# Three accumulators of softmax sums joined on POOL before TensorE reduces them

## The chip, the cores and the metric

The kernel runs on one core of a Trainium2 chip. The metric is the device time of one execution in microseconds (us). The engines are TensorE (PE; its weight loads are PEld), VectorE (DVE), ScalarE (ACT), GpSimd (POOL) and SyncE (SP, which here only issues DMAs).

## What is computed

A block of three residual steps on x of shape (2, 2048, 512), in float32: half a feed-forward layer with sign weights, self-attention with 16 heads of 32, half a feed-forward layer again. Each step normalizes first.

```python
def attn(x):                      # per batch element, 16 heads, HEAD_DIM 32
    q, k, v = proj(w_q), proj(w_k), proj(w_v)
    scores = einsum('bhqd,bhkd->bhqk', q, k) * SCALE
    probs = softmax(scores, axis=-1)
    attn = einsum('bhqk,bhkd->bhqd', probs, v)
    return einsum('bsd,ed->bse', attn, w_o)

x = x + 0.5 * ffn(layernorm(x))   # relu(x @ sign(up).T * up_scale) @ sign(down).T * down_scale
x = x + attn(layernorm(x))
x = x + 0.5 * ffn(layernorm(x))
```

## The kernel before

The stages follow each other: first feed-forward (up to about 620 us), projections to q, k, v (to about 865 us), attention (to about 2540 us), output projection and second feed-forward. The change lies in attention.

Attention runs over NH = 32 heads (16 for each of two batch elements), H in the code. A head has 2048 keys in KT = 16 tiles of 128 (kt) and 2048 queries in QC = 4 chunks of 512 (q). The work is written transposed: a score matmul (`scores`, L802) has 128 keys on the partitions and 512 queries along the row. ACT takes the exponential (L786, in `scalar_tile`) into a slot `prob[kt % 8]` of 128x2048; a slot is 1 MB, and there are PR = 8. The maxima that are subtracted come from a second matmul of the same size (`maxima`, L806), whose results DVE reduces (L737); this runs LEAD = 4 tiles ahead, so that tiles 12 to 15 of a head's loop already make maxima for the head after next. At tile TURN = 13 the maxima are transposed by PE (L822), split by DVE and written by SP into two rows of the q tile (`max_rows`).

The order on PE is written by hand in `tensor_group`: a group u is two key tiles, G = 2, so a head has 8 groups. A group is 8 score matmuls and 8 maxima matmuls in turn, and then the output matmuls (`out_tile`, L830) of the two tiles before: for each tile four matmuls with v, one for each chunk, 32 columns wide, which work side by side into the four quarters of one bank. The last two tiles of head H - 1 are thus multiplied in group 0 of head H.

Besides its output a head needs the sum of its probabilities over all keys. Three accumulators of 128x2048 share the 16 tiles: POOL adds tiles 0, 2, 4, ..., 14 and 15 into `acc` (`add`, L710); tiles 1, 5, 9, 13 go by DMA into the first of `dma_acc`, tiles 3, 7, 11 into the second (`move`: the first of each is a plain copy, L722, the later ones accumulate, L725). POOL issues these DMAs between its additions, in the order of the tiles, so they share one queue. ACT writes a slot again 8 tiles later and waits (`tile_free`) until the addition or the DMA that read it is done. The accumulators are double buffered by the parity of H.

What is left is the sum over the 128 partitions. PE makes it with a matrix of ones in `sums`: four matmuls on `acc` (L846) and four on each of the two DMA accumulators (L851). It runs once a head, for head H - 1, at the end of group SUMS_AFTER = 2 of head H. It takes one of the four banks that the maxima use in turn. ACT copies this bank to `head_total` (`copy_sums`, L228) at tile 6, after the second of the tile's four exponentials; PE may use the bank again only then (`bank_free`, semaphore `sums_copied`). SP sends the sums through DRAM to turn them (`move_sums`), DVE inverts them at tile 12 (`invert`, L255), SP stores them (`store_inverse`).

At the start of each head SP waits for the last output matmuls of the head before (`head_free`) and then loads q, k and v of head H + 2: four of q and k high parts, two low parts, and v, 256 KB each (L679, L681).

The last head (31) is different: fewer tiles on POOL and DMA, some tiles multiplied by ones directly (L837), and in between the first output projection products. There DVE, at tile 6, waits for `t_ready` of head 30 and then runs the first normalization steps of the last stage (L83, L85, L87, L89), which PE's mean matmuls at the end of group 3 need.

Of the kernel before, what the change touches and what calls it, by code (L numbers as in the profile page):

```python
# [6 lines left out]
ALU = mybir.AluOpType  # L7
# [9 lines left out]
CH = 512  # L17
# [3 lines left out]
KT = SEQ // P  # L21
QC = SEQ // CH
NH = BATCH * HEADS
# [557 lines left out]
LEAD, G = 4, 2  # L581
# [3 lines left out]
UNITS = KT * QC  # L585
S_BANK, S_FREED = bank_order(UNITS, SR, (23, 46))
AHEAD = LEAD * QC
SUMS_AFTER = 2
SUMS_AT, TURN_AT = QC * G * (SUMS_AFTER + 1), QC * 7 * G
SLOTS = UNITS + 2  # L590
CHAINS = 2
# [26 lines left out]
def direct(H):  # L618
    return tuple(kt for kt in range(KT) if kt not in pooled(H) and kt not in moved(H))
# [13 lines left out]
def all_adds(H):  # L633
    return adds_to(H, pooled(H)[-1])


def all_moves(H, x):
    return moves_to(H, moved(H)[x::CHAINS][-1])


class Attention:
# [3 lines left out]
    def __init__(self, c, qk_parts, v_scr, head_out, ident, ones_sum):  # L645
        self.nc, self.qk_parts, self.v_scr, self.head_out, self.ident, self.ones_sum = c.nc, qk_parts, v_scr, head_out, ident, ones_sum
        self.q_st = [c.sb(f"att_q{i}", at, [P, SEQ], F32R) for i, at in enumerate((OUT_AT, HID_LO_AT, X0_AT))]
        self.k_st = [c.sb(f"att_k{i}", at, [P, SEQ], F32R) for i, at in enumerate((HID_HI_AT, INV_B_AT, RAW_AT))]
        self.v_st = [c.sb(f"att_v{i}", at, [P, KT, HD]) for i, at in enumerate((HID_AT + 2, HID_AT, INV_AT))]
        self.prob = [c.sb(f"att_p{i}", BIG_AT + 8 * i, [P, SEQ]) for i in range(PR)]  # L650
        self.acc = [c.sb(f"att_acc{i}", at, [P, SEQ]) for i, at in enumerate((CENT_AT, HI1_AT))]
        self.dma_acc = [[c.sb(f"att_dma_acc{i}_{x}", at, [P, SEQ]) for x, at in enumerate(ats)]
                        for i, ats in enumerate(((WORK_AT, SUM_AT), (LO1_AT, X1_AT)))]
        self.row_max = [c.sb(f"att_row_max{i}", HEAD_AT + 4 + 0.25 * i, [P, KT, QC]) for i in range(2)]
        self.neg_max = c.sb("att_neg_max", HEAD_AT + 4.5, [P, KT])
        self.neg_hi, self.neg_lo = c.sb("att_neg_hi", HEAD_AT + 5, [KT, P], F32R), c.sb("att_neg_lo", HEAD_AT + 5.5, [KT, P], F32R)
        self.m_ps, self.s_ps, self.o_ps = c.bank[0:4], c.bank[4:7], c.bank[7]
        self.loaded = [c.sem(f"att_loaded{i}") for i in range(NB)]
        self.ones_set = c.sem("att_ones_set")
        self.m_ready, self.m_read = c.sem("att_m_ready"), c.sem("att_m_read")  # L660
        self.neg_dve, self.neg_pe, self.neg_loaded = c.sem("att_neg_dve"), c.sem("att_neg_pe"), c.sem("att_neg_loaded")
        self.s_ready, self.exp_done, self.p_used = c.sem("att_s_ready"), c.sem("att_exp_done"), c.sem("att_p_used")
        self.summed, self.dma_summed = c.sem("att_summed"), [c.sem(f"att_dma_summed{x}") for x in range(CHAINS)]
        self.move_begun, self.t_ready = c.sem("att_move_begun"), c.sem("att_t_ready")

    def sums_bank(self, H):
# [45 lines left out]
    def move(self, pool, H, kt):  # L712
# [10 lines left out]
        else:  # L723
            pool.sem_inc(self.move_begun, 1)
            self.nc.gpsimd.dma_start(into[:], self.prob[kt % PR][:], accum_op=ALU.add).then_inc(self.dma_summed[x], 16)  # L725

    def pool_tile(self, pool, H, kt):
        if kt in pooled(H) and kt != pooled(H)[0]:
            self.add(pool, H, kt)
        elif kt in moved(H):  # L730
            self.move(pool, H, kt)
# [24 lines left out]
    def vector_tile(self, dve, H, kt):  # L756
        T = H + 1 + (kt + LEAD) // KT
        for q in range(QC):
            p = QC * kt + q
            if T < NH:  # L760
                self.reduce_block(dve, UNITS * (H + 1) + AHEAD + p, self.m_ps[m_bank(H, slot(p))], T % 2, (kt + LEAD) % KT, q)
            if kt == TURN - 1 and q == 0 and H + 1 < NH:
                self.negate(dve, H + 1)
        if kt == TURN and H + 1 < NH:
            self.rows_out(dve, H + 1, self.turn_bank(H))
        if H > 0 and kt == 12:
            self.head_out.invert(dve, H - 1)


# [11 lines left out]

    def scalar_tile(self, act, H, kt):
        self.tile_free(act, H, kt)
        for q in range(QC):
            act.wait_ge(self.s_ready, UNITS * H + QC * kt + q + 1)
            self.nc.scalar.activation(self.prob[kt % PR][:, q * CH:(q + 1) * CH], self.s_ps[S_BANK[kt * QC + q]][:], ACT.Exp,  # L786
                                      scale=SCALE).then_inc(self.exp_done, 1)
            if q == 1 and H > 0:
                if kt == G:
                    act.wait_ge(self.p_used, KT * H)  # L790
                    self.head_out.copy_out(act, H - 1, self.o_ps)
                if kt == G * (SUMS_AFTER + 1):
                    act.wait_ge(self.t_ready, H)
                    self.head_out.copy_sums(act, H - 1, self.sums_bank(H - 1))

# [41 lines left out]
        ins.then_inc(self.p_used, 1)  # L839

    def sums(self, pe, H):
        out, first = self.sums_bank(H), not direct(H)
        pe.wait_ge(self.summed, all_adds(H))
        for q in range(QC):
            rows = slice(q * HD, (q + 1) * HD)
            self.nc.tensor.matmul(out[rows, :], self.ones_sum[:], self.acc[H % 2][:, q * CH:(q + 1) * CH], start=first, stop=False)  # L846
        for x in range(CHAINS):
            pe.wait_ge(self.dma_summed[x], 16 * all_moves(H, x))
            for q in range(QC):
                rows = slice(q * HD, (q + 1) * HD)  # L850
                ins = self.nc.tensor.matmul(out[rows, :], self.ones_sum[:], self.dma_acc[H % 2][x][:, q * CH:(q + 1) * CH],  # L851
                                            start=False, stop=(x == CHAINS - 1))
        ins.then_inc(self.t_ready, 1)

    def bank_free(self, pe, H, at):
# [49 lines left out]
def macaron_kernel(nc, xT, w_qT, w_kT, w_vT, w_oT, upT, downT, up_scale, down_scale, output_scale, outT):  # L905
    ctx = ExitStack()
    with ctx:
# [18 lines left out]
        c = Chip(nc, ctx)  # L926
# [20 lines left out]
        with nc.Block() as block:  # L947
            @block.sync
            def _(sp):
# [37 lines left out]
                for H in range(NH):  # L987
                    if H > 0:
                        att.head_free(sp, H)
                    if H + 2 < NH:  # L990
                        att.load(sp, H + 2)
                    if H == 0:
                        sp.dma_start(wo_raw[:], w_oT).then_inc(wo_loaded, 16)
                    if H == LAST - 1:
                        oproj.load(sp, 0)
                        st.load(sp, 2 * NCH, x1)
                    if H == LAST:
                        signs2.load(sp, 0)
                        oproj.load(sp, 1)
                    if H > 0:  # L1000
                        head_out.store_out(sp, H - 1)
                        head_out.move_sums(sp, H - 1)
                        head_out.store_inverse(sp, H - 1)
                    if H < LAST:
                        att.max_rows(sp, H + 1)

                sp.wait_ge(oproj.scaled, 2)
                signs2.load(sp, 4)
# [22 lines left out]
            @block.gpsimd  # L1031
            def _(pool):
                nc.gpsimd.memset(f32(ones_mean[:]), 1.0 / D)
                nc.gpsimd.memset(ones_sum[:], 1.0)
                nc.gpsimd.memset(ident[:], 0.0).then_inc(const_set, 1)
                pool.wait_ge(const_set, 1)
                nc.gpsimd.affine_select(out=ident[:], in_=ident[:], compare_op=ALU.not_equal, fill=1.0,
                                        base=0, pattern=[[-1, P]], channel_multiplier=1).then_inc(const_set, 1)
                pool.wait_ge(ffn1.hid_used, NCH * HT)
                for b in (0, 1):  # L1040
                    att.set_ones(b)
                qkv.all_stored(pool, NCH)
                att.set_ones(2)
                pool.wait_ge(att.ones_set, NB)

                for H in range(NH):
                    for kt in range(KT):
                        att.pool_tile(pool, H, kt)
                        if H == 1 and kt == 9:
                            pool.wait_ge(wo_done, 1)  # L1050
                            nc.gpsimd.tensor_tensor(flat(wo[1][:]), flat(wo_raw[:]), flat(f32(wo[0][:])), ALU.subtract).then_inc(wo_done, 1)
                        if H == LAST - 1 and kt == 8:
                            oproj.pool_scale(pool, 0)
                        if H == LAST - 1 and kt == 11:
                            oproj.pool_split_lo(pool, 0)
                        if H == LAST and kt == 5:
                            oproj.pool_scale(pool, 1)
# [183 lines left out]
```

## Time and profile before

| | |
|---|---|
| median of 3 runs | 3118.62 us (3116.81 to 3118.83) |
| profiled execution: time / span | 3113.91 us / 3112.0 us |
| mean granted TensorE clock | 0.986 |
| PE busy | 2973.2 us (96%) |
| DVE busy | 2038.0 us (65%) |
| ACT busy | 1613.9 us (52%) |
| POOL busy | 1331.3 us (43%) |
| DMA | 428.54 MB, mean 138 GB/s |

The profile is of one execution. Busy is the time in which an engine has at least one instruction at work, and the shares are means over all stages. A granted clock of 1.00 is 2.4 GHz. Instructions that only issue DMAs are not counted as busy, though they take POOL's time. A DMA's landing time is counted from the start of its issue.

### The profile page before, as it was taken

How to read it: one execution, taken by the hardware profiler on the slowest of the kernel's cores; microseconds unless marked ns; L12 is line 12 of the kernel's file. 1: busy time of each engine (PE TensorE's matmuls, PEld its weight loads, DVE VectorE, ACT ScalarE, POOL GpSimd, SP SyncE). 2: the span in 40 equal slices, each digit the busy share in tenths (PEclk: the TensorE clock that was granted, in tenths of full speed). 3: DMA queues.
4: the chain of work that ended last, by engine and by line, in shares of the span. 5: the costliest groups of instructions: out<-in, count | busy, mean ns of one | idle time of the engine just before them, and what ended most of it. 6: DMA issues, size and time to landing. Idle time of an engine off the chain costs nothing.

```text
span 3112.0 us, 38839 instructions
## 1 busy us (share of the span) xinstructions
PE 2973.2 (96%) x14768; PEld 1964.9 (63%) x14768; DVE 2038.0 (65%) x3044; ACT 1613.9 (52%) x2851; POOL 1331.3 (43%) x489
## 2 busy tenths in 40 slices
PE   6999999998799999999999999999999889999998
PEld 4888887876555555555555555555555447888887
DVE  4555556766587777777787777787877234555552
ACT  5344443322166666666666666666666553333333
POOL 0000000000078787878787878788888700000000
PEclk9999999999899999999999999999999989999999
DMA  4110012563287888888888787878787754222200
GB/s 141 62 55 28 28 55 88 186 214 119 84 203 170 192 179 195 177 192 177 190 177 193 174 197 172 200 173 197 178 194 181 192 148 120 57 55 54 55 28 28
DMA packets 184891, 428.54 MB, mean 138 GB/s; under 512 B 89728, under 2 KB 90752, under 8 KB 148224
## 3 DMA queue, kind: packets, MB, share of 16 engines
q0 software_dynamic: 32400, 235.94, 32.7%
q1 hardware_dynamic: 152304, 190.11, 22.0%
q8 instruction: 116, 1.90, 0.3%
q14 instruction: 71, 0.58, 0.1%
HBM read 121.91 MB, written 67.63 MB: 61 GB/s over the span
## 4 chain that ended last, share of the span: by engine, by line
PE 71%; ACT 9%; DMA 6%; DVE 5%; POOL 4%; issue 4%; SPq 0%; ACTq 0%; POOLq 0%; DVEq 0%
PE bank L426 15%; PE bank L445 15%; PE bank L830 12%; PE bank L802 9%; PE bank L553 8%; ACT att_p L786 8%; PE bank L806 6%; DMA att_dma_acc<-att_p 5%; POOL att_acc L710 4%; PE bank L317 3%; DVE att_row_max L737 2%; PE bank L851 2%; PE bank L846 1%; DVE norm_inv L108 1%; ACT head_total L228 0%
## 5 line engine op out<-in xcount | busy, mean ns | idle before, releaser
L737 DVE TENSOR_REDUCE att_row_max<-bank 128x1 f32<-128x512 f32 x2048 | 1258.5, 683 | 383.5 <-PE bank L806 379.9
L786 ACT ACTIVATE att_p<-bank 128x512 f32<-128x512 f32 x2048 | 1047.0, 620 | 585.2 <-PE bank L802 573.2
L710 POOL TENSOR_TENSOR att_acc<-att_acc,att_p 128x2048 f32<-128x2048 f32 x217 | 993.4, 4578 | 222.9 <-ACT att_p L786 218.4
L802 PE MATMUL bank<-att_q,att_k 98*128 98x512 f32 x2048 | 852.7, 418 | 30.2 <-ACT att_p L786 25.6
L806 PE MATMUL bank<-att_k,att_q 96*128 96x512 f32 x2048 | 815.9, 400 | 48.8 <-DVE att_row_max L737 38.0
L802 PEld LDWEIGHTS bank<-att_q,att_k 98*128 98x128 f32 x2048 | 385.9, 189 | 403.1 <-issue 210.2
L830 PE MATMUL bank<-att_p,att_v 128*32 128x512 f32 x4096 | 502.1, 608 | 0.0
L806 PEld LDWEIGHTS bank<-att_k,att_q 96*128 96x128 f32 x2048 | 390.5, 191 | 123.6 <-DVE att_row_max L737 45.3
L369 DVE TENSOR_TENSOR ffn_hid_lo<-ffn_hid,ffn_hid_hi 128x512 fp32r<-128x512 f32 x256 | 176.1, 688 | 430.7 <-ACT ffn_hid_hi L404 412.8
L401 ACT ACTIVATE ffn_hid<-bank,up_s 128x512 f32<-128x512 f32 x256 | 176.1, 688 | 474.8 <-PE bank L426 474.2
L426 PE MATMUL bank<-hi,ffn_up_w 128*128 128x512 f32 x1024 | 402.7, 393 | 20.3 <-DVE lo L122 15.3
L426 PE MATMUL bank<-lo,ffn_up_w 128*128 128x512 f32 x1024 | 401.8, 392 | 0.0
L445 PE MATMUL bank<-ffn_hid_hi,ffn_down_w 128*128 128x512 f32 x1024 | 399.7, 390 | 1.9 <-DVE ffn_hid_lo L369 1.9
L445 PE MATMUL bank<-ffn_hid_lo,ffn_down_w 128*128 128x512 f32 x1024 | 399.6, 390 | 0.0
L698 POOL MEMSET att_k<- 2x2048 f32 x3 | 5.3, 1801 | 858.3 <-PE bank L445 506.2
L830 PEld LDWEIGHTS bank<-att_p,att_v 128*32 128x32 f32 x4096 | 108.0, 110 | 243.6 <-ACT att_p L786 136.7
L426 PEld LDWEIGHTS bank<-hi,ffn_up_w 128*128 128x128 f32 x1024 | 194.2, 190 | 63.8 <-DVE lo L122 13.0
L426 PEld LDWEIGHTS bank<-lo,ffn_up_w 128*128 128x128 f32 x1024 | 194.4, 190 | 41.0
L445 PEld LDWEIGHTS bank<-ffn_hid_hi,ffn_down_w 128*128 128x128 f32 x1024 | 192.7, 188 | 43.0 <-DVE ffn_hid_lo L369 2.4
L445 PEld LDWEIGHTS bank<-ffn_hid_lo,ffn_down_w 128*128 128x128 f32 x1024 | 192.8, 188 | 40.6
L710 POOL TENSOR_TENSOR att_acc<-att_p,att_p 128x2048 f32<-128x2048 f32 x32 | 146.5, 4579 | 74.9 <-ACT att_p L786 74.9
L404 ACT ACTIVATE ffn_hid_hi<-bank,up_s 128x512 fp32r<-128x512 f32 x256 | 174.6, 682 | 0.0
(89 smaller groups left out, 2215.9 us busy)
## 6 DMA issues: line engine op xcount, KB each, us to landing
att_dma_acc<-att_p POOLq DMA_DIRECT2D x225, 1024.0 KB, 7.6
x<-x_after_ffn SPq DMA_DIRECT2D x16, 1024.0 KB, 7.4
att_q<-q_hi SPq DMA_DIRECT2D x64, 256.0 KB, 4.2
att_k<-k_hi SPq DMA_DIRECT2D x64, 256.0 KB, 8.9
x<-xT SPq DMA_DIRECT2D x8, 1024.0 KB, 7.1
x_after_ffn<-x_out SPq DMA_DIRECT2D x8, 1024.0 KB, 9.3
q_hi<-qkv_o_hi SPq DMA_DIRECT2D x32, 256.0 KB, 2.0
q_lo<-qkv_o_lo SPq DMA_DIRECT2D x32, 256.0 KB, 2.5
```

Source lines behind the costliest of these rows:

```text
L369: nc.vector.tensor_tensor(self.hid_lo[:, ht % RING, :], self.hid[:, ht % RAW, :], f32(self.hid_hi[:, ht % RING, :]), ALU.subtract).then_in ...
L401: nc.scalar.activation(self.hid[:, ht % RAW, :], self.up_ps[ht % 2][:], ACT.Relu, scale=self.vecs["up"][:, ht:ht + 1])
L404: nc.scalar.activation(self.hid_hi[:, ht % RING, :], self.up_ps[ht % 2][:], ACT.Relu, scale=self.vecs["up"][:, ht:ht + 1]).then_inc(self.u ...
L426: ins = nc.tensor.matmul(self.up_ps[ht % 2][:], signs.up[:, ht // 4, dt, ht % 4 * P:(ht % 4 + 1) * P], part[N % 2][:, dt, :], start=(dt == ...
L445: ins = nc.tensor.matmul(self.down_ps[dt][:], signs.down[:, h, dt * P:(dt + 1) * P], part[:, h % RING, :], start=(h == 0 and i == 0), stop ...
L553: ins = self.nc.tensor.matmul(self.out_ps[t % QR][:], left, right, start=(dt == 0 and (a, b) == (0, 0)), stop=(dt == DT - 1 and (a, b) == ...
L710: self.nc.gpsimd.tensor_tensor(self.acc[H % 2][:], a[:], self.prob[kt % PR][:], ALU.add).then_inc(self.summed, 1)
L737: self.nc.vector.tensor_reduce(self.row_max[odd][:, qt, q:q + 1], m[:], axis=AX.X, op=ALU.max).then_inc(self.m_read, 1)
L786: self.nc.scalar.activation(self.prob[kt % PR][:, q * CH:(q + 1) * CH], self.s_ps[S_BANK[kt * QC + q]][:], ACT.Exp, scale=SCALE).then_inc( ...
L802: self.nc.tensor.matmul(self.s_ps[S_BANK[i]][:], self.k_st[H % NB][0:KM, kt * P:(kt + 1) * P], self.q_st[H % NB][0:KM, q * CH:(q + 1) * CH ...
L806: self.nc.tensor.matmul(m[:], self.q_st[T % NB][0:KQ, qt * P:(qt + 1) * P], self.k_st[T % NB][0:KQ, q * CH:(q + 1) * CH], start=True, stop ...
L830: ins = self.nc.tensor.matmul(self.o_ps[rows, :], self.v_st[H % NB][:, kt, :], self.prob[kt % PR][:, q * CH:(q + 1) * CH], start=(kt == 0) ...
```

## The change

The three accumulators of a head are made one before PE reduces them, in heads 0 to 30. After a head's last tile POOL issues one more accumulating DMA that adds the second DMA accumulator to the first (`join_chains`, at tile 0 of the next head), and after tile 3 it waits for it and adds the result to its own accumulator (`join`). PE then multiplies only `acc` by ones, four matmuls instead of twelve. The last head keeps its way. The sums move from the end of group 2 to that of group 3; ACT copies their bank ahead of tile 8's exponentials instead of inside those of tile 6; DVE inverts at tile 14 instead of 12; SP stores the inverse after the maxima rows instead of ahead of them.

```diff
-SUMS_AFTER = 2
+SUMS_AFTER = 3
...
+    def join_chains(self, pool, H):
+
+        for x in range(CHAINS):
+            pool.wait_ge(self.dma_summed[x], 16 * all_moves(H, x))
+        if H > 0:
+            pool.wait_ge(self.chains_joined, 16 * H)
+        first, second = self.dma_acc[H % 2]
+        pool.sem_inc(self.move_begun, 1)
+        self.nc.gpsimd.dma_start(first[:], second[:], accum_op=ALU.add).then_inc(self.chains_joined, 16)
+
+    def join(self, pool, H):
+
+        pool.wait_ge(self.chains_joined, 16 * (H + 1))
+        pool.wait_ge(self.summed, all_adds(H))
+        acc = self.acc[H % 2]
+        self.nc.gpsimd.tensor_tensor(acc[:], acc[:], self.dma_acc[H % 2][0][:], ALU.add).then_inc(self.joined, 1)
...
-        if H > 0 and kt == 12:
+        if H > 0 and kt == 14:
             self.head_out.invert(dve, H - 1)
...
     def scalar_tile(self, act, H, kt):
         self.tile_free(act, H, kt)
+        if H > 0 and kt == G * (SUMS_AFTER + 1):
+            act.wait_ge(self.t_ready, H)
+            self.head_out.copy_sums(act, H - 1, self.sums_bank(H - 1))
         for q in range(QC):
...
-                if kt == G * (SUMS_AFTER + 1):
-                    act.wait_ge(self.t_ready, H)
-                    self.head_out.copy_sums(act, H - 1, self.sums_bank(H - 1))
...
     def sums(self, pe, H):
-        out, first = self.sums_bank(H), not direct(H)
-        pe.wait_ge(self.summed, all_adds(H))
+        out, first, last = self.sums_bank(H), not direct(H), H == NH - 1
+        if last:
+            pe.wait_ge(self.summed, all_adds(H))
+        else:
+            pe.wait_ge(self.joined, H + 1)
         for q in range(QC):
...
-        for x in range(CHAINS):
+        for x in range(CHAINS if last else 0):
...
                     if H > 0:
                         head_out.store_out(sp, H - 1)
                         head_out.move_sums(sp, H - 1)
-                        head_out.store_inverse(sp, H - 1)
                     if H < LAST:
                         att.max_rows(sp, H + 1)
+                    if H > 0:
+                        head_out.store_inverse(sp, H - 1)
...
                 for H in range(NH):
                     for kt in range(KT):
+                        if H > 0 and kt == 0:
+                            att.join_chains(pool, H - 1)
                         att.pool_tile(pool, H, kt)
+                        if H > 0 and kt == 3:
+                            att.join(pool, H - 1)
```

The order of instructions on POOL from tile 14 of an even head to tile 5 of the next, before. `att_p_93` to `att_p_100` are the eight slots; `att_acc_101`, `att_dma_acc_0_103` and `att_dma_acc_1_104` belong to even heads, 102, 105 and 106 to odd ones:

```order
L710 TENSOR_TENSOR att_acc_101<-att_acc_101,att_p_99 128x2048
L710 TENSOR_TENSOR att_acc_101<-att_acc_101,att_p_100 128x2048
L722 DMA att_dma_acc_0_105<-att_p_94 128x2048
L710 TENSOR_TENSOR att_acc_102<-att_p_93,att_p_95 128x2048
L722 DMA att_dma_acc_1_106<-att_p_96 128x2048
L710 TENSOR_TENSOR att_acc_102<-att_acc_102,att_p_97 128x2048
L725 DMA att_dma_acc_0_105<-att_p_98 128x2048
```

The same stretch with the change:

```order
L711 TENSOR_TENSOR att_acc_101<-att_acc_101,att_p_99 128x2048
L711 TENSOR_TENSOR att_acc_101<-att_acc_101,att_p_100 128x2048
L736 DMA att_dma_acc_0_103<-att_dma_acc_1_104 128x2048
L723 DMA att_dma_acc_0_105<-att_p_94 128x2048
L711 TENSOR_TENSOR att_acc_102<-att_p_93,att_p_95 128x2048
L723 DMA att_dma_acc_1_106<-att_p_96 128x2048
L743 TENSOR_TENSOR att_acc_101<-att_acc_101,att_dma_acc_0_103 128x2048
L711 TENSOR_TENSOR att_acc_102<-att_acc_102,att_p_97 128x2048
L726 DMA att_dma_acc_0_105<-att_p_98 128x2048
```

The joining DMA (L736) stands ahead of tile 1's copy in the queue, and the joining addition (L743) ahead of tile 4's.

PE around an even head's sums, before (end of group 2, with the output matmuls of tiles 2 and 3 ahead, and the next group behind):

```order
L806 MATMUL bank<-att_k_87,att_q_84 128x512
L830 MATMUL bank<-att_p_95,att_v_92 32x512 x4
L830 MATMUL bank<-att_p_96,att_v_92 32x512 x4
L846 MATMUL bank<-att_acc_101,ones_sum 32x512 x4
L851 MATMUL bank<-att_dma_acc_0_103,ones_sum 32x512 x4
L851 MATMUL bank<-att_dma_acc_1_104,ones_sum 32x512 x4
L802 MATMUL bank<-att_q_86,att_k_89 128x512
```

With the change (end of group 3, with tiles 4 and 5 ahead):

```order
L823 MATMUL bank<-att_k_87,att_q_84 128x512
L847 MATMUL bank<-att_p_97,att_v_92 32x512 x4
L847 MATMUL bank<-att_p_98,att_v_92 32x512 x4
L866 MATMUL bank<-att_acc_101,ones_sum 32x512 x4
L819 MATMUL bank<-att_q_86,att_k_89 128x512
```

The eight matmuls on the DMA accumulators are gone, and the four that are left stand one group later.

## Rows read from the trace of the kernel before

**Rows 1.** The page, part 1: busy us (share of the span) xinstructions.

```profile
PE 2973.2 (96%) x14768; PEld 1964.9 (63%) x14768; DVE 2038.0 (65%) x3044; ACT 1613.9 (52%) x2851; POOL 1331.3 (43%) x489
```

**Rows 2.** Busy by stretch: stretch, us, each engine's busy us, PEclk, DMA share, GB/s.

```profile
968.91:2404.90 1435.99, 1409.93 (x7870) 762.07 (x7869) 1114.06 (x1904) 936.28 (x1848) 1170.30 (x422) 1.00 0.81 186
```

**Rows 3.** Timeline of PE, 1543 to 1560 us: start us, us, instruction [idle before <-releaser].

```profile
1543.23 1.92 PE L830 MATMUL bank<-att_p,att_v 128*32 128x512 f32 x16
1544.98 1.04 PE L846 MATMUL bank<-att_acc,ones_sum 128*32 128x512 f32 x8
1545.84 1.90 PE L851 MATMUL bank<-att_dma_acc,ones_sum 128*32 128x512 f32 x16
1547.66 0.50 PE L802 MATMUL bank<-att_q,att_k 98*128 98x512 f32 x1
...
1549.91 0.50 PE L806 MATMUL bank<-att_k,att_q 96*128 96x512 f32 x1 [0.33 <-ACT head_total L228]
...
1552.21 1.92 PE L830 MATMUL bank<-att_p,att_v 128*32 128x512 f32 x16
...
1558.01 1.92 PE L830 MATMUL bank<-att_p,att_v 128*32 128x512 f32 x16
```

**Rows 4.** The chain that ended last, 1518 to 1547 us: start us, us, what.

```profile
1518.26 0.16 DVE head_inv_t L255
...
1545.16 0.86 PE bank L846 x8
1546.02 1.72 PE bank L851 x16
```

**Rows 5.** Timeline of POOL, tile 14 of a head to tile 5 of the next.

```profile
1523.85 9.29 POOL L710 TENSOR_TENSOR att_acc<-att_acc,att_p 128x2048 f32<-128x2048 f32 x2 [0.82 <-ACT att_p L786]
1533.10 0.60 POOL L722 DMA_DIRECT2D att_dma_acc<-att_p  x1
1535.88 4.58 POOL L710 TENSOR_TENSOR att_acc<-att_p,att_p 128x2048 f32<-128x2048 f32 x1 [2.19 <-ACT att_p L786]
1540.40 0.59 POOL L722 DMA_DIRECT2D att_dma_acc<-att_p  x1
1541.62 4.56 POOL L710 TENSOR_TENSOR att_acc<-att_acc,att_p 128x2048 f32<-128x2048 f32 x1 [0.63 <-ACT att_p L786]
1546.14 0.88 POOL L725 DMA_DIRECT2D att_dma_acc<-att_p  x1
```

**Rows 6.** Timeline of POOL in head 30, where two extra operations keep it busy.

```profile
2428.69 4.58 POOL L710 TENSOR_TENSOR att_acc<-att_acc,att_p 128x2048 f32<-128x2048 f32 x1 [0.50 <-ACT att_p L786]
2433.24 4.52 POOL L289 TENSOR_TENSOR op_raw<-op_raw,op_inv_first 128x2048 f32<-128x2048 f32 x1
2437.71 0.87 POOL L725 DMA_DIRECT2D att_dma_acc<-att_p  x1
2438.32 4.83 POOL L710 TENSOR_TENSOR att_acc<-att_acc,att_p 128x2048 f32<-128x2048 f32 x1
2443.14 0.88 POOL L725 DMA_DIRECT2D att_dma_acc<-att_p  x1
```

**Rows 7.** Line L722, 968 to 2405 us: the 57 plain copies of tiles 1 and 3.

```profile
DMA to landing us min/median/max: 7.9/9.2/11.9
```

**Rows 8.** Line L725, 968 to 2405 us: the 140 accumulating DMAs.

```profile
DMA to landing us min/median/max: 6.8/7.3/10.2
```

**Rows 9.** DMA issues, 2466.7 to 2466.9 us: head 31's first copy, without loads beside it.

```profile
att_dma_acc<-att_p POOLq DMA_DIRECT2D x1, 1024.0 KB, 5.1
```

**Rows 10.** Timeline of SP, 1532.5 to 1536.5 us: the first of a head's loads.

```profile
1532.80 0.79 SPq L679 DMA_DIRECT2D att_q<-q_hi  x2
```

**Rows 11.** Busy by stretch, columns as in rows 2: after the next head's loads.

```profile
1586.00:1599.00 13.00, 12.69 (x82) 5.51 (x80) 8.41 (x14) 7.15 (x15) 10.52 (x4) 1.00 1.05 280
```

**Rows 12.** Timeline of DVE in head 31: the first normalization steps.

```profile
2493.47 1.23 DVE L83 TENSOR_TENSOR norm_work<-x 128x1024 f32<-128x1024 f32 x1
...
2495.92 0.69 DVE L89 TENSOR_TENSOR norm_sum_lo<-norm_sum,norm_sum_hi 128x512 fp32r<-128x512 f32 x1
```

More of the change, by code:

```diff
@@ L663, in __init__ @@
         self.summed, self.dma_summed = c.sem("att_summed"), [c.sem(f"att_dma_summed{x}") for x in range(CHAINS)]
+        self.chains_joined, self.joined = c.sem("att_chains_joined"), c.sem("att_joined")
         self.move_begun, self.t_ready = c.sem("att_move_begun"), c.sem("att_t_ready")
@@ L787, in scalar_tile @@
                                       scale=SCALE).then_inc(self.exp_done, 1)
[L788 to L791, printed above, removed]
-                if kt == G * (SUMS_AFTER + 1):
-                    act.wait_ge(self.t_ready, H)
-                    self.head_out.copy_sums(act, H - 1, self.sums_bank(H - 1))
+            if q == 1 and H > 0 and kt == G:
+                act.wait_ge(self.p_used, KT * H)
+                self.head_out.copy_out(act, H - 1, self.o_ps)
     def scores(self, pe, H, kt, q):
@@ L841, in sums @@
     def sums(self, pe, H):
-        out, first = self.sums_bank(H), not direct(H)
-        pe.wait_ge(self.summed, all_adds(H))
+        out, first, last = self.sums_bank(H), not direct(H), H == NH - 1
[3 more added lines that the diff above has]
+            pe.wait_ge(self.joined, H + 1)
         for q in range(QC):
             rows = slice(q * HD, (q + 1) * HD)
-            self.nc.tensor.matmul(out[rows, :], self.ones_sum[:], self.acc[H % 2][:, q * CH:(q + 1) * CH], start=first, stop=False)
-        for x in range(CHAINS):
+            ins = self.nc.tensor.matmul(out[rows, :], self.ones_sum[:], self.acc[H % 2][:, q * CH:(q + 1) * CH],
+                                        start=first, stop=not last)
+        for x in range(CHAINS if last else 0):
             pe.wait_ge(self.dma_summed[x], 16 * all_moves(H, x))
@@ L851, in sums @@
                 ins = self.nc.tensor.matmul(out[rows, :], self.ones_sum[:], self.dma_acc[H % 2][x][:, q * CH:(q + 1) * CH],
-                                            start=False, stop=(x == CHAINS - 1))
+                                            start=False, stop=(x == CHAINS - 1 or not last))
         ins.then_inc(self.t_ready, 1)
```

## The prediction

> **What bounds the kernel now.** I read the page's busy shares first: TensorE (PE) is busy 96% of the span, POOL 43% [rows 1]. The shares are a mean over five stages, and the change touches one, so I read the attention stage alone. From the first plain copy of head 2 to that of head 30 lie 28 heads in 1435.99 us, or 51.29 us each; in them PE is busy 1409.93 us (98%) and POOL 1170.30 us (81%), the granted clock is 1.00 and the DMA engines are busy 0.81 [rows 2]. So PE sets the period, and POOL, which looks idle on the page, has only about ten microseconds to spare in a head.
>
> Next the timeline of PE around one head's sums. The reader should see a group of two key tiles as a block that ends in the L830 matmuls. From the L830 block at 1552.21 to the one at 1558.01 it is 5.80 us, a plain group; from 1543.23 to 1552.21, the group ahead of which the sums stand, it is 8.98 us [rows 3]. The extra 3.18 us are the price of the sums. The chain of waits splits it: 0.86 us for the four matmuls on the POOL accumulator and 1.72 us for the eight on the two DMA accumulators [rows 4]; the other 0.60 us are around PE's wait for the copy of the sums' bank at 1549.91 [rows 3], since ScalarE (ACT) copies that bank only after two exponentials of the next tile.
>
> Last, POOL's timeline of the same head. POOL adds an even tile in 4.6 us and then issues a DMA for the odd one; most of its gaps end with an ACT tile, so POOL waits for its input. Only the two adds of tiles 14 and 15 run back to back; they end at 1533.1, and a plain copy of tile 1 follows at once [rows 5].
>
> **The change, part by part.** *Removed on PE:* the eight matmuls of L851 in heads 0 to 30, 1.72 us a head. *Copy of the sums moved ahead of the tile's exponentials:* ACT is idle there (the wait before is for PE), so the 0.60 us wait mostly goes; between 0.3 and 0.6, I take 0.60, since the copy can start with the end of the sums, when ACT's next input is still in the making. *The reciprocal moved from tile 12 to 14:* it takes 0.16 us of the chain that ends in the transpose [rows 4]; after tile 14 no transpose waits for VectorE (DVE). Between 0 and 0.16; I take 0.16. *SP's order:* the rows of maxima now go ahead of the store of the inverse, which was early anyhow: 0. The sums a group later: 0 in itself. PE alone would then need 51.29 - 1.72 - 0.60 - 0.16 = 48.81 us a head.
>
> *Added on POOL and its queue:* one accumulating DMA, one addition of the same shape as the others, and between them a wait for the DMA to land. What stands behind that wait is tile 4's addition, and with it all of POOL's program. I therefore work out POOL's own period, from the start of one joining addition to that of the next. It needs POOL's pace when nothing holds it: one addition to the next is 2433.24 - 2428.69 = 4.55 us, and a DMA with the addition behind it 2443.14 - 2437.71 = 5.43 us [rows 6]. From the joining addition to the next joining DMA there are: the joining addition and tile 4, two of 4.55; five pairs of DMA and addition (tiles 5 and 6 up to 13 and 14), 27.15; tile 15, 4.55. Sum 40.80 us. Then the joining DMA runs, D us from its issue to its landing, with tile 1's copy, tile 2's addition and tile 3's copy (6 us together) hidden under it; and about 0.1 us until POOL goes on. **POOL's period is 40.9 + D.** It passes PE's 48.8 when D is over 7.9, and today's 51.29 when D is over 10.4. So the verdict hangs on D.
>
> *What D is.* No row of the kernel before shows an accumulate at this place, so I bound it. The place is bad: the joining DMA is issued where tile 1's copy is now, at 1533.1 [rows 5], and at 1532.80 SP has begun to issue the seven loads for the head after next [rows 10]; in the 13 us that follow them the DMA share is 1.05, which is full [rows 11]. The plain copies of tiles 1 and 3, all under those loads, land after 7.9 to 11.9 us, 9.2 in the median [rows 7]. The accumulates, most of them at quieter times, land after 6.8 at least and 7.3 in the median [rows 8], and a plain copy with little beside it after 5.1 [rows 9]. Accumulating thus costs 6.8 - 5.1 = 1.7 us over a plain copy, and loads about 4.1 (9.2 - 5.1). Both together give 10.9. I take 11.4, since a longer transfer meets more of the full stretch. Lower end 7.3 (as if there were no loads), upper end 11.9 + 1.7 = 13.6. It is nearest to rows 7, which have the very place, so D is more likely above 10 than under it.
>
> The Trainium skill, "DMA: Bandwidth & Descriptors", section "Anatomy of one DMA — SWDGE (gpsimd) path", gives a fit of about 2.0 us and the bytes over 436 KB per us; for 1 MB that is an estimate of 4.4 us. The trace is above it in every row here, 5.1 for a plain copy [rows 9] and 6.8 for the quickest accumulate [rows 8]; by the page the join would be hidden wholly and the time would be that of the first rival, 3046 us, against my 3147.
>
> *The sum.* POOL's period is 40.9 + 11.4 = 52.3 us, 1.0 over today's. In the first joined head there is still room: the DMA from 1533.1 would land at 1544.5 and the addition end at 1549.1, while PE comes to the sums at about 1550.9 (the L830 block of that group ends near 1554.1, less the 2.58 of sums that no longer stand ahead and less 0.60). That head gains 2.35 us up to the group behind its sums. POOL then falls behind by 52.3 - 48.8 = 3.5 us a head, eats the slack of 1.8 at once, and PE waits at the sums: 29 intervals (sums of head 0 to sums of head 29) at +1.0, or +29.3 us. Head 1 has POOL's extra subtraction for the output weights both before and after, head 30 has two extra POOL operations but PE's products too, which leave POOL time; I put both at nothing beyond this.
>
> *The last head.* DVE begins the normalization of the last stage only after t_ready, at tile 6. The sums are now at the end of that very group, and PE's mean matmuls come right behind them and need four DVE steps, from 2493.47 to 2496.61, or 3.1 us [rows 12]; what the removed matmuls give there is 1.72. Net +1.5 us.
>
> Together: -2.35 + 29.3 + 1.5 = +28.5 us. The profiled execution took 3113.91 us (span 3112.0), 0.15% under the median of 3118.62; its sum comes to 3142, and against the median I forecast **3147 us**. A measurement can tell about 0.2% (6 us) from no change here.
>
> **Rivals.**
> 1. *PE stays the bound, faster.* If the joining DMA lands within 7.9 us, everything on POOL is hidden: 29 x 2.48 = 72 us and the first head's 2.35 are gained, 1.5 lost: 3046 us. For it: quiet accumulates need 7.3 [rows 8]. Against it: the place, where no copy of the 57 landed under 7.9, and those only copied [rows 7]. The price is decided at D = 7.9, the sign at 10.4. Chance 0.10.
> 2. *POOL is the bound, yet faster.* At D = 9.2, as a plain copy there, the period is 50.1, 1.19 less than now: 29 x 1.19 = 34.5, so 3083 us. For it: POOL falls behind PE, so the joining DMA comes later against the loads, past part of them. Against it: tile 3's copy, 7 us later, is among the same 57. Chance 0.17; within 0.2% of no change, D 10.2 to 10.6: 0.08.
> 3. *A slot of probabilities comes free late.* Tile 1's copy stands behind the joining DMA in one queue; ACT needs its slot at tile 9, about 18 us after the issue. With 11.4 for the join and 4 to 5 for the copy that just holds. If it doesn't, each us of lateness is another 29: at 1.5 us, 3190 us. Chance 0.09.
> The forecast itself, D of 10.6 to 13: 0.56.
>
> **How the numbers follow.** Slower: 0.56 + 0.09 = 0.65; same 0.08; faster 0.10 + 0.17 = 0.27. The range: low end at D = 8.8 (period 49.7, 29 x -1.6 and the ends: 3072), which leaves out rival 1 and a little; high end at D = 12.9 (period 53.8, +72: 3190).
>
> **What would show it.** Right: the joining DMAs land after 10.5 to 12.5 us; POOL is idle before its joining addition, some 5 us a head, ended by that DMA, and nowhere else in the head; PE shows an idle time before the sums of 3 to 4 us a head where there was none; the period is about 52.3; the wait for the bank's copy has gone; DVE and ACT wait longer with nothing changed in their durations. Wrong in the favourable way: POOL still waits for ACT in most gaps and PE's period is near 48.8. If ACT waits for a DMA at tile 9, it is rival 3. If POOL's additions themselves got longer than 4.6 us, or POOL's unheld pace is not the one of rows 6, the sum 40.8 is what fails.

## The result and the profile after

The changed kernel takes 3166.08 us in the median of 4 runs (3165.47 to 3167.75), the kernel before 3118.66. The ratio is 1.0154, with a 95% interval of 1.0137 to 1.0172: slower by 47 us, where +28 was forecast with a range up to 3190.

| | before | after |
|---|---|---|
| profiled execution: time / span | 3113.91 / 3112.0 us | 3165.47 / 3163.5 us |
| mean granted TensorE clock | 0.986 | 0.970 |
| PE busy | 2973.2 us | 2960.1 us |
| POOL busy | 1331.3 us | 1505.0 us |
| DMA | 428.54 MB | 460.99 MB |
| a head, mean of 28 between the transposes of maxima in heads 1 and 29 | 51.28 us | 52.88 us |

The page of the changed kernel, first part 1, then the engines of part 4, the chain that ended last:

```profile
PE 2960.1 (94%) x14272; PEld 1968.5 (62%) x14272; DVE 2041.0 (65%) x3044; ACT 1622.1 (51%) x2851; POOL 1505.0 (48%) x551
...
PE 57%; POOL 17%; issue 10%; DMA 8%; ACT 5%; DVE 3%; SPq 0%; POOLq 0%; ACTq 0%; DVEq 0%
```

PE has less to do [rows 1], yet all takes longer. In the chain PE's share is 57% where it was 71% before, POOL's 17% where it was 4%. Busy shares alone would never tell this, since POOL's is still 48%.

The busy times of the changed kernel from the first plain copy of head 2 to that of head 30, columns as in rows 2:

```profile
973.00:2448.10 1475.10, 1393.63 (x7389) 763.39 (x7388) 1112.49 (x1897) 939.80 (x1840) 1327.58 (x477) 0.97 0.86 200
```

The 28 heads take 1475.10 us against 1435.99 [rows 2]. POOL has 47.4 us of busy time in a head of 52.7. The rest, 5.3 us, is one idle time. The line of the joining DMA (L736) and who waited for it:

```profile
  POOL att_acc L743: 153.1, 30
...
DMA to landing us min/median/max: 6.9/11.6/13.6
```

It lands 11.6 us after its issue in the median, and the joining addition waits for it 153.1 us in 30 heads, 5.1 a head. POOL's timeline at such a place answers to rows 5:

```profile
1496.22 4.59 POOL L711 TENSOR_TENSOR att_acc<-att_acc,att_p 128x2048 f32<-128x2048 f32 x1 [0.43 <-ACT att_p L807]
1500.74 0.88 POOL L736 DMA_DIRECT2D att_dma_acc<-att_dma_acc  x1
1501.33 0.85 POOL L723 DMA_DIRECT2D att_dma_acc<-att_p  x1
1501.89 4.89 POOL L711 TENSOR_TENSOR att_acc<-att_p,att_p 128x2048 f32<-128x2048 f32 x1
1506.44 0.83 POOL L723 DMA_DIRECT2D att_dma_acc<-att_p  x1
1512.10 4.50 POOL L743 TENSOR_TENSOR att_acc<-att_acc,att_dma_acc 128x2048 f32<-128x2048 f32 x1 [4.83 <-DMA att_dma_acc<-att_dma_acc]
1516.57 4.55 POOL L711 TENSOR_TENSOR att_acc<-att_acc,att_p 128x2048 f32<-128x2048 f32 x1
...
1553.07 0.84 POOL L736 DMA_DIRECT2D att_dma_acc<-att_dma_acc  x1
```

Tile 15's addition ends, the joining DMA goes out at 1500.74, 11.4 us later the joining addition starts, and 40.97 us after that start the next joining DMA goes out (41.04 in the mean of 27 heads). Nearly none of POOL's additions now waits for ACT: in these 28 heads such waits come to 1.0 us, where they were 262. POOL is the bound.

PE at the same sums, then at those of the next head:

```profile
1511.34 1.92 PE L847 MATMUL bank<-att_p,att_v 128*32 128x512 f32 x16
1516.74 1.07 PE L866 MATMUL bank<-att_acc,ones_sum 128*32 128x512 f32 x8 [3.48 <-POOL att_acc L743]
1517.74 0.79 PE L819 MATMUL bank<-att_q,att_k 98*128 98x512 f32 x1
1518.33 0.63 PE L823 MATMUL bank<-att_k,att_q 96*128 96x512 f32 x1
1518.76 0.63 PE L819 MATMUL bank<-att_q,att_k 98*128 98x512 f32 x1
...
1570.08 1.07 PE L866 MATMUL bank<-att_acc,ones_sum 128*32 128x512 f32 x8 [0.17 <-POOL att_acc L743]
```

PE waits 3.48 us for the joining addition, and then its matmuls come every 0.43 us instead of every 0.23: the clock has dropped to the lower of its two levels, 1.2 GHz. The busy times of that stretch show the granted clock (third column from the right), and those of the next stretch show it full again:

```profile
1516.74:1524.76 8.02, 8.02 (x25) 5.27 (x25) 4.79 (x7) 4.96 (x9) 8.02 (x3) 0.57 0.33 67
1524.76:1532.00 7.24, 7.09 (x45) 3.70 (x48) 5.36 (x10) 4.51 (x9) 7.24 (x4) 1.00 0.96 199
```

In the next head PE comes to the sums late enough to wait only 0.17 us, and keeps its clock. So heads alternate: the transposes stand 55.65 us apart, then 50.35, 55.67, 49.97, while the joining additions in the same heads stand 52.5 to 53.2 apart. Whether the lower clock costs time is a question for the experiments.

### The profile page after: what moved, and what is told of

The parts are those of the page before. It is cut to its first block, busy times and chain, and to the rows that moved or that the text cites. A ratio compares the mean times of both kernels' runs of the same rounds, so it can differ in the third digit from the quotient of the medians.

```text
span 3163.5 us, 38001 instructions
## 1 busy us (share of the span) xinstructions
PE 2960.1 (94%) x14272; PEld 1968.5 (62%) x14272; DVE 2041.0 (65%) x3044; ACT 1622.1 (51%) x2851; POOL 1505.0 (48%) x551
## 2 busy tenths in 40 slices
DMA packets 189352, 460.99 MB, mean 146 GB/s; under 512 B 90224, under 2 KB 91248, under 8 KB 148720
## 4 chain that ended last, share of the span: by engine, by line
PE 57%; POOL 17%; issue 10%; DMA 8%; ACT 5%; DVE 3%; SPq 0%; POOLq 0%; ACTq 0%; DVEq 0%
PE bank L426 15%; PE bank L445 14%; POOL att_acc L711 12%; PE bank L553 8%; DMA att_dma_acc<-att_p 6%; PE bank L819 6%; PE bank L847 6%; PE bank L823 5%; ACT att_p L807 4%; POOL att_acc L743 3%; PE bank L317 3%; POOL att_dma_acc L723 1%; PE bank L866 1%; DVE att_row_max L755 1%; DVE norm_inv L108 1%
## 5 line engine op out<-in xcount | busy, mean ns | idle before, releaser
L711 POOL TENSOR_TENSOR att_acc<-att_acc,att_p 128x2048 f32<-128x2048 f32 x217 | 1084.4, 4997 | 8.7 <-ACT att_p L807 4.5
L819 PE MATMUL bank<-att_q,att_k 98*128 98x512 f32 x2048 | 875.0, 430 | 41.7 <-ACT att_p L807 30.0
L823 PE MATMUL bank<-att_k,att_q 96*128 96x512 f32 x2048 | 830.7, 407 | 38.8 <-DVE att_row_max L755 38.4
L819 PEld LDWEIGHTS bank<-att_q,att_k 98*128 98x128 f32 x2048 | 398.2, 195 | 435.0 <-issue 205.3
L823 PEld LDWEIGHTS bank<-att_k,att_q 96*128 96x128 f32 x2048 | 402.5, 197 | 102.2 <-DVE att_row_max L755 45.7
L726 POOL DMA_DIRECT2D att_dma_acc<-att_p x161 | 210.3, 1306 | 18.1 <-ACT att_p L807 17.1
L743 POOL TENSOR_TENSOR att_acc<-att_acc,att_dma_acc 128x2048 f32<-128x2048 f32 x31 | 140.6, 4536 | 153.1 <-DMA att_dma_acc<-att_dma_acc 153.1
## 6 DMA issues: line engine op xcount, KB each, us to landing
att_dma_acc<-att_dma_acc POOLq DMA_DIRECT2D x31, 1024.0 KB, 11.6
```

The source lines that it names most:

```text
L711: self.nc.gpsimd.tensor_tensor(self.acc[H % 2][:], a[:], self.prob[kt % PR][:], ALU.add).then_inc(self.summed, 1)
L743: self.nc.gpsimd.tensor_tensor(acc[:], acc[:], self.dma_acc[H % 2][0][:], ALU.add).then_inc(self.joined, 1)
L819: self.nc.tensor.matmul(self.s_ps[S_BANK[i]][:], self.k_st[H % NB][0:KM, kt * P:(kt + 1) * P], self.q_st[H % NB][0:KM, q * CH:(q + 1) * CH ...
L823: self.nc.tensor.matmul(m[:], self.q_st[T % NB][0:KQ, qt * P:(qt + 1) * P], self.k_st[T % NB][0:KQ, q * CH:(q + 1) * CH], start=True, stop ...
```

## The experiments

The theories, as the expectations name them. A: the period of the changed kernel is POOL's, that is the time from the joining addition to the next joining DMA (41.0 us) and that DMA's landing. B: the loss comes from the moved sums and copies. C: POOL has too much to add, whatever it waits for. D: the added megabyte per head delays other transfers. E: PE's stalls and the clock after them set the pace. "Before" in the ratios is the kernel before, run on the same chip: 3114.78 us beside the first four kernels, 3114.24 beside the others. Periods are means of 28 heads between transposes, as in the table above.

### The order alone

Edit: no join at all, and PE multiplies all three accumulators; the rest of the change stays.

```diff
-        out, first, last = self.sums_bank(H), not direct(H), H == NH - 1
+        out, first, last = self.sums_bank(H), not direct(H), True
...
-                        if H > 0 and kt == 0:
-                            att.join_chains(pool, H - 1)
                         att.pool_tile(pool, H, kt)
-                        if H > 0 and kt == 3:
-                            att.join(pool, H - 1)
```

> Only the order of the change is kept: sums after group 3, the bank copied ahead of tile 8's exponentials, the reciprocal at tile 14, the store of the inverse last. Nothing is joined, and PE multiplies all three accumulators. Theory A (POOL's period, with the wait for the joining DMA in it, sets the pace of the changed kernel): that wait is gone, PE is the bound, and a head takes 51.3 - 0.60 - 0.16 = 50.5 us, less 21 us in 28 heads, and 3 to 5 us are lost in the last head: 3100 us (3093 to 3108). Theory B (the loss comes from the later sums or the moved copies): 3150 or more.

Measured: 3098.28 us, ratio 0.9955 (0.9941 to 0.9969), period 50.67. The moved copy and the reciprocal are worth 0.62 us a head, against 0.76 in the prediction. POOL waits for its input again, as this line of the waits, 960 to 2400 us, shows (us in total, times, longest):

```profile
POOL att_acc L711 <- ACT att_p L807: 248.7, 199, 3.4
```

B falls.

### The addition alone, and the DMA alone

Edit of the first: POOL's joining addition takes the first DMA accumulator as it is, with no joining DMA, and PE multiplies two accumulators.

```diff
-        pool.wait_ge(self.chains_joined, 16 * (H + 1))
+        pool.wait_ge(self.dma_summed[0], 16 * all_moves(H, 0))
...
-        for x in range(CHAINS if last else 0):
+        for x in range(0 if last else 1, CHAINS):
...
-                        if H > 0 and kt == 0:
-                            att.join_chains(pool, H - 1)
```

> No joining DMA: after tile 3 POOL adds the first DMA accumulator to its own, and PE multiplies this and the second DMA accumulator, eight matmuls. POOL does all of its added arithmetic and waits for nothing new. Theory A: POOL needs about 41 us from joining addition to tile 15 and 6 us for tiles 1 to 3, 47 in all, under PE's 48.8 + 0.86 = 49.7 us, so PE is the bound: 28 x 1.6 = 45 us gained, some 5 lost at the end, 3079 us (3070 to 3090). Theory C (POOL's added work is too much whatever it waits for): POOL without idle time and 3140 or more.

Edit of the second: the joining DMA runs, the joining addition is left out, and PE waits for the DMA itself.

```diff
-        if last:
-            pe.wait_ge(self.summed, all_adds(H))
-        else:
-            pe.wait_ge(self.joined, H + 1)
+        pe.wait_ge(self.summed, all_adds(H))
...
+        for x in range(CHAINS if last else 1):
+            if last:
+                pe.wait_ge(self.dma_summed[x], 16 * all_moves(H, x))
+            else:
+                pe.wait_ge(self.chains_joined, 16 * (H + 1))
...
-                        if H > 0 and kt == 3:
-                            att.join(pool, H - 1)
```

> The joining DMA runs as in the change, but POOL does not add its result: PE waits for the DMA at the sums and multiplies POOL's accumulator and the joined one, eight matmuls. The megabyte more in each head is there, POOL's wait is not. Theory A: PE is the bound at 49.7 us a head, 3079 us (3070 to 3090), though the joining DMA lands after 10 to 12 us as before. Theory D (the added traffic delays other transfers, and PE or ACT wait for those): 3120 or more, with waits of ACT for DMAs or of PE for the rows of maxima.

Measured: the addition alone 3071.26 us, ratio 0.9867 (0.9851 to 0.9884), period 49.83; the DMA alone 3074.97 us, ratio 0.9876 (0.9862 to 0.9891), period 49.84. In the first the waits of POOL's additions for ACT are less than before but there, in the second the joining DMA lands as late as in the change:

```profile
POOL att_acc L711 <- ACT att_p L807: 84.8, 62, 2.4
```

```profile
DMA to landing us min/median/max: 6.9/12.1/13.1
```

Each of these two kernels is faster than the kernel before by some 40 us, about what the order (28 x 0.62 us) and the four matmuls fewer (28 x 0.86 us) give; both halves together make it slower by 47. Neither POOL's arithmetic nor the traffic is the cost. It is that one waits for the other on POOL. C and, for this size of traffic, D fall.

### The loads behind the joining DMA

Edit: one wait on SP, in each head after the first.

```diff
+                    if 0 < H and H + 2 < NH:
+                        sp.wait_ge(att.chains_joined, 16 * H)
                     if H + 2 < NH:
                         att.load(sp, H + 2)
```

> The changed kernel with one wait more on SP: the loads for the head after next are issued only when the joining DMA has landed. Theory A: without the loads beside it the joining DMA lands after about 7 us instead of 11.6, POOL's period falls from 52.7 to 41.1 + 7.1 = 48.2, PE's 48.8 is the bound: 28 x 2.45 = 69 us gained over the kernel before and 6 to 10 lost at the end, 3057 us (3045 to 3075). If the landing is long for its own reasons (an accumulate from an accumulator), it stays near 11 and the time near 3166.

Measured: 3107.85 us, ratio 0.9972 (0.9952 to 0.9992), with a wide scatter (3094 to 3124), period 50.60. The landing came out as foreseen, the time did not. The landings of the joining DMA, and then two lines of the waits, 960 to 2400 us:

```profile
DMA to landing us min/median/max: 6.8/6.9/12.3
```

```profile
PE bank L819 <- DMA att_v<-v_rows: 19.0, 7, 3.1
PE bank L819 <- DMA att_q<-att_neg_lo: 14.2, 19, 1.7
```

With nothing beside it the joining DMA needs 6.9 us instead of 11.6, so the loads are what made it slow, and POOL's wait is nearly gone (9.5 us in all). But the loads now start some 8 us later in a head, while the DMA engines are busy 0.93 of the time over the 28 heads, and in some heads PE stands before tile 12 and waits for v (3.06 us in a head of 54.5 us). Most heads took 49 to 50 us. A wait was traded for another: PE waits for delayed transfers here, as in D. Whether the later start alone does it or the added megabyte too is not shown.

### More of the landing exposed, and less

Edits: the tile after which the joining addition stands, 1 in one kernel and 4 in another, instead of 3.

```diff
-                        if H > 0 and kt == 3:
+                        if H > 0 and kt == 1:
                             att.join(pool, H - 1)
```

> The changed kernel with the joining addition after tile 1 instead of tile 3, so that tile 2's addition and tile 3's copy no longer run under the joining DMA. Theory A: POOL's period is what stands between joining addition and next joining DMA, now 41.0 + 4.55 + 0.9 = 46.4, and the landing of about 11.6: 58.0 us a head, 6.7 more than in the kernel before, 28 times, and about 12 at the ends: 3320 us (3280 to 3350). Theory E (PE's stalls and its lower clock after them set the pace, the landing only triggers them): a few us more than 3166, as PE waits once a head in both.

> The changed kernel with the joining addition after tile 4, so that tile 4's addition runs under the joining DMA too. Theory A: POOL's period is 36.5 + 12 = 48.5 us, no longer the bound. But the joining addition can't end before about 24 us into the head, since tile 4's addition waits for its exponentials, and PE comes to the sums at that very time; PE's period is 48.9 with stalls of 0 to 0.5: 3060 us (3048 to 3085), of it 5 to 10 us of loss in the last two heads. Theory E: stalls of PE remain in each head and with them a period over 51.

Measured after tile 1: 3314.46 us, ratio 1.0648 (1.0625 to 1.067), period 57.60. The landings and POOL's wait for them:

```profile
  POOL att_acc L743: 306.9, 31
...
DMA to landing us min/median/max: 6.9/11.2/14.0
```

46.4 + 11.2 = 57.6, which is the period measured. Theory E expected a few us more than 3166, and the run took 148 more. PE's clock was low once a head here too (0.95 over the span), and the sum holds without a term for it: while POOL is the bound, PE's slow group fits in the time in which it would have waited.

Measured after tile 4: 3065.73 us, ratio 0.9855 (0.9835 to 0.9876), period 49.52. The DMA lands after 12.6 us in the median, later than in the changed kernel, and it hardly matters, as POOL's and PE's timelines of one head show:

```profile
1510.83 0.86 POOL L736 DMA_DIRECT2D att_dma_acc<-att_dma_acc  x1
...
1524.19 4.56 POOL L743 TENSOR_TENSOR att_acc<-att_acc,att_dma_acc 128x2048 f32<-128x2048 f32 x1 [0.81 <-DMA att_dma_acc<-att_dma_acc]
```

```profile
1528.89 1.06 PE L866 MATMUL bank<-att_acc,ones_sum 128*32 128x512 f32 x8 [0.74 <-POOL att_acc L743]
```

A single character, the place of the joining addition (tile 4 instead of 3), is worth 100 us. What is left is a short wait at the sums, 8.7 us in 13 of these heads.

### The last head

Edit: head 30 keeps three accumulators, and its sums stay at the end of group 2 of head 31.

```diff
+def sums_after(H):
+    return 2 if H == NH - 1 else SUMS_AFTER
...
-        out, first, last = self.sums_bank(H), not direct(H), H == NH - 1
+        out, first, last = self.sums_bank(H), not direct(H), H >= NH - 2
...
-                        if H > 0 and kt == 3:
+                        if 0 < H < NH - 1 and kt == 3:
                             att.join(pool, H - 1)
```

The places that used SUMS_AFTER for group and copy use `sums_after(H)`, and the joining DMA has the same condition as the addition.

> The changed kernel, but head 30 keeps its three accumulators and its sums after group 2 of the last head, as before the change. It tells what the last head costs: if the 5 us that the last head lost in the changed kernel come from the four normalization steps behind the later sums, 3160 us (3157 to 3163); if they come from elsewhere, no change against 3166.

Measured: 3161.16 us (3159.21 to 3167.32; the changed kernel 3166.08), ratio to before 1.0163 (1.0143 to 1.0183). The total shows nothing: the changed kernel's ratio to its own runs of the kernel before is 1.0154, and the ranges overlap. That 3161 came where 3160 was expected is luck: in the profiled execution the gain of the last head was lost again in head 30, whose joining DMA, which the edit does not touch, landed after 15.3 us and not 12.4. That head took 70.8 us between transposes instead of 63.8.

```profile
2461.31 4.48 POOL L747 TENSOR_TENSOR att_acc<-att_acc,att_dma_acc 128x2048 f32<-128x2048 f32 x1 [8.84 <-DMA att_dma_acc<-att_dma_acc]
```

Against the changed kernel this one was 4.6 us ahead at the transpose in head 29, lost 6.9 in head 30 and gained 5.5 in the last head. Only the stretch that the edit changes answers the question. From the last transpose to the first matmul of the second feed-forward layer it is 92.8 us before, 98.2 with the change (2495.1 to 2593.3) and 92.7 here (2497.5 to 2590.2). PE's rows behind the sums in the changed kernel show why:

```profile
2542.23 1.04 PE L866 MATMUL bank<-att_acc,ones_sum 128*32 128x512 f32 x8
2546.59 0.50 PE L141 MATMUL bank<-norm_sum_hi,ones_mean 128*128 128x512 f32 x1 [3.32 <-DVE norm_sum_lo L89]
...
2547.16 0.87 PE L819 MATMUL bank<-att_q,att_k 98*128 98x512 f32 x3
...
2551.02 3.64 PE L847 MATMUL bank<-att_p,att_v 128*32 128x512 f32 x16
```

PE waits 3.32 us for the four DVE steps, and the output matmuls after that take 3.64 us instead of 1.92 at the lower clock. Here PE is the bound, so the clock does cost.

### A candidate

Edit: the joining addition after tile 4, SUMS_AFTER = 4, and the last head as in the kernel of the section above (e7).

> A candidate: the joining addition after tile 4, the sums after group 4, head 30 unjoined as in e7. Theory A: POOL's period 48.5, PE's 48.8 and no stall, since the joined accumulator is ready some 5 us before the sums: 28 x 2.45 = 69 us gained, nothing lost in the last head: 3048 us (3040 to 3060), faster than both kernels and than the addition alone (3071). Theory D (the DMA queue, 8 MB a head, becomes late for the probability slots or the maxima rows): ACT or PE waits for DMAs and 3070 or more.

Measured: 3053.87 us (3048.93 to 3056.21), ratio 0.9812 (0.9794 to 0.9831), period 49.24. It is faster than both kernels, by 60 us against the kernel before and some 110 against the changed one, and faster than the addition alone. Its busy times over 28 heads, and a line of its waits:

```profile
973.00:2350.00 1377.00, 1355.51 (x7418) 741.24 (x7417) 1110.39 (x1903) 934.45 (x1847) 1330.15 (x476) 1.00 0.92 215
```

```profile
PEld bank L823 <- DMA att_q<-att_neg_lo: 25.7, 23, 2.0
```

POOL is busy 97% of the time and PE 98%, at full clock, and the DMA engines 92%. Most heads take 49.0 us, where 48.8 was worked out; one of 50.2 us has a wait of 1.08 us for the maxima rows at its start. The 25.7 us above are waits of PE's weight loads for these rows, which largely overlap with running matmuls; PE itself waits 5.5 us for them, in 10 of the heads. These rows land after 5.0 us here, 2.5 in the kernel before, with the DMA engines busy 0.92 of the time and not 0.81.

## Why the prediction was right, point by point

**The mechanism.** POOL's own period was worked out and found over PE's, and this held in each of its parts. POOL waits once a head and for the joining DMA alone, 5.1 us; the wait of PE stands before the sums; the wait for the bank's copy is gone. The terms: joining addition to next joining DMA 40.80 predicted, 41.04 measured in the mean. The landing 11.4 predicted, 11.6 measured. The period 52.3 predicted; the starts of the joining additions of heads 2 and 29, 984.06 and 2406.54, give 52.68. The experiments turned the landing's place (tile 1, 3, 4) and its length (the loads), and the period followed each time, down to where PE is the bound; no part of the change alone gave the loss. One sign of being wrong did appear and misleads: POOL's additions are recorded as longer, 5.0 us in the mean where they were 4.6. The prediction named that as what would break its 40.8, and yet start to start the stretch takes 41.04, since the longer rows overlap with their neighbours.

**PE without POOL.** 48.81 us was predicted as PE's own period. The candidate's heads without a wait take 49.0, and the order alone gave 0.62 of the 0.76 us.

**Too small by 19 us** against the medians (23 on the profiled executions, where the change is -4.0 us at the transpose in head 1, +40.5 at that in head 29, +45.6 at the last one and +51.0 at the second feed-forward layer). The steps that were off, all of them sizes:
- The period, by 0.38 us, of which POOL's path from the joining addition on has 0.24 and the landing 0.16: 10 us in 27 heads by the joining additions, 12 by the transposes in heads 2 and 29 (+1.2 and +40.5 against the kernel before).
- Head 1, whose extra subtraction for the output weights the prediction put "at nothing beyond this" because it is there both before and after. Before, it fell into POOL's slack; now it stands in the path that sets the pace. In head 1 it is 45.65 us from joining addition to next joining DMA, and 57.34 us to the next joining addition, 5.0 more than the 52.3 of the sum. At the transpose in head 2 the change is thus 1.2 us behind the kernel before, where the sum has it 1.3 ahead. The row of the subtraction:

```profile
946.67 5.54 POOL L1077 TENSOR_TENSOR wo_lo<-wo_raw,wo_hi 128x2048 fp32r<-128x2048 f32 x1
```

- Head 30, which the prediction put "at nothing beyond this" since PE's products would leave POOL time. POOL comes to its two extra operations late, and ACT's split and PE's scores stand behind the first. The two rows of the changed kernel (ACT, then PE), and those of the kernel before:

```profile
2484.47 1.91 ACT L302 ACTIVATE hi<-op_raw 128x2048 fp32r<-128x2048 f32 x1 [10.18 <-POOL op_raw L289]
...
2486.92 0.80 PE L819 MATMUL bank<-att_q,att_k 98*128 98x512 f32 x1 [12.24 <-ACT att_p L807]
```

```profile
2437.80 1.91 ACT L302 ACTIVATE hi<-op_raw 128x2048 fp32r<-128x2048 f32 x1 [3.38 <-POOL op_raw L289]
...
2440.24 0.79 PE L802 MATMUL bank<-att_q,att_k 98*128 98x512 f32 x1 [5.44 <-ACT att_p L786]
```

The wait grew by 6.8 us, and the head by 5.1, where 1.0 was in the sum. An engine that runs late hands its lateness to whoever depends on its other work.
- The last head, +1.5 predicted and +5.4 measured; the lower clock behind the stall makes about 1.7 of the difference in the output matmuls alone, and the rest was not taken apart.

Together these are 12 + 2.5 + 4 + 4 = 22.5 us, nearly all of the gap of the profiled executions. All four err the same way, so nothing cancelled in the forecast.

**The rivals.** That the DMA would land within 7.9 us needs it to be alone, as the kernel with the delayed loads shows (6.9); in the change it was not. The fit of the Trainium skill, "DMA: Bandwidth & Descriptors", section "Anatomy of one DMA — SWDGE (gpsimd) path" (an estimate of 4.4 us for 1 MB), is under each of the landings here: 5.1 us for a plain copy with no loads beside it [rows 9], 6.9 for the joining DMA alone and 11.6 under loads. That POOL is the bound and yet faster needed 9.2 us. No late slot of probabilities was seen: the plain copies behind the joining DMA landed after 13.1 us in the median, where it was 9.2 [rows 7], and ACT waited for none of them; once in these heads, for 1.8 us, it waited for an addition.

**Not foreseen:** PE's wait at the sums is 62.5 us in 28 heads, 2.2 a head and not 3 to 4, since the slow matmuls after a stall use up part of it: PE ran 88.7 us of these heads at 1.2 GHz, which cost it half of that, 1.6 us a head; and PE now and then waits for the rows of maxima.

## What to carry to other kernels

Before work is moved to an engine that looks idle, write down that engine's own period, from one fixed instruction to the same one in the next round, with every wait in it; a DMA that the engine issues and waits for itself counts with its landing less what stands between issue and wait. Take the landing from the place where it will be, with the transfers that start there. Then put the wait behind as much of the engine's other work as its reader allows, and move the reader too.

## What the runs showed of the hardware

- Behind a stall of PE of 3.48 us the granted clock was 0.57 for 8.0 us (1516.74), matmuls 0.43 us apart and not 0.23, and 1.00 in the stretch after; behind a wait of 0.17 us in the next head it stayed high. Of the changed kernel's 28 waits at the sums the 12 up to 1.98 us left the clock at 1.00, and 15 of the 16 from 2.15 us on have a stretch at 1.2 GHz; the one of 3.03 us has none. While POOL was the bound this cost nothing in the total, as the sum for tile 1 shows, and heads often alternated between 50 and 55.6 us.
- One accumulating DMA of 1 MB from SBUF to SBUF landed after 6.9 us with no loads beside it and after 11.6 with 1.75 MB of loads.
- POOL's accumulating DMA issues took 0.87 us where POOL had waited before, and up to 1.6 us where it ran without a break, with the next addition beginning under them; additions took 5.3 us there instead of 4.6. From one issue to the next it was nevertheless 5.1 to 5.5 us, so durations of overlapping rows should not be summed; start-to-start distances can.
